# The first norm of a Swin block kernel placed in front of the preparation of all weights, with own buffers and a second queue for the loads

## The reference

```python
xl = roll(layernorm(x over channels) * n1w + n1b, (-3, -3))
xw = windows of 7 x 7 tokens                      # 16 * 64 windows of 49 tokens
q, k, v = xw @ qkv_w.T + qkv_b                    # 6 heads of 32
out = softmax(q k^T * 32**-0.5) v
out = out @ proj_w.T + proj_b                     # windows undone, rolled back
h = layernorm(out) * n2w + n2b
h = gelu(h @ fc1_w.T + fc1_b) @ fc2_w.T + fc2_b   # hidden size 768
return h + x
```

## Time and profile before

| | |
|---|---|
| median of 3 runs | 3201.64 us |
| the profiled execution | 3201.47 us |
| its span, first to last instruction | 3199.7 us |
| mean granted TensorE clock, of full speed | 0.998 |
| busy: PE, ACT, DVE, POOL | 98%, 93%, 78%, 32% |
| chain of work that ended last | PE 97%, DVE 1%, SP's queue 1%, ACT 1% |
| bytes moved by DMA | 129.30 MB, mean 40 GB/s |

### The profile page before, as it was taken

How to read it: one execution, slowest core, us unless ns; L and a number is a source line. 1 busy time by engine, 2 the same in 40 slices (tenths; PEclk the granted TensorE clock), 3 DMA queues, 4 the chain that set the end, 5 groups by cost and what they waited for, 6 DMA issues and landing times.

```text
span 3199.7 us, 76844 instructions
## 1 busy us (share of the span) xinstructions
PE 3133.7 (98%) x28076; PEld 3046.4 (95%) x28076; DVE 2501.2 (78%) x7214; ACT 2978.5 (93%) x5498; POOL 1019.0 (32%) x1288
## 2 busy tenths in 40 slices
PE   3999999999999999999999999999999999999998
PEld 3899999999999999999999999999999999999998
DVE  4787788788778878877887887787788788778876
ACT  1899999999999999999999999999999999999997
POOL 0233333333333333333333333333333333323332
PEclk9999999999999999999999999999999999999999
DMA  2112112111211211121121121112111111211211
GB/s 63 21 40 46 38 39 43 42 38 40 46 37 39 43 42 38 41 45 37 39 44 41 39 43 42 38 40 46 38 39 43 42 38 40 46 37 39 43 33 28
DMA packets 458709, 129.30 MB, mean 40 GB/s; under 512 B 392803, under 2 KB 458084, under 8 KB 458340
## 3 DMA queue, kind: packets, MB, share of 16 engines
q1 hardware_dynamic: 458340, 124.39, 18.4%
HBM read 47.20 MB, written 38.54 MB: 27 GB/s over the span
## 4 chain that ended last, share of the span: by engine, by line
PE 97%; DVE 1%; SPq 1%; ACT 1%; DMA 0%; issue 0%; POOL 0%; POOLq 0%; DVEq 0%; ACTq 0%
PE psum L547 8%; PE psum L304 7%; PE psum L306 6%; PE psum L305 6%; PE psum L307 6%; PE psum L308 6%; PE psum L526 6%; PE psum L517 4%; PE psum L506 4%; PE psum L507 4%; PE psum L508 4%; PE psum L518 4%; PE psum L480 4%; PE psum L532 4%; PE psum L314 3%; PE psum L318 3%
## 5 line engine op out<-in xcount | busy, mean ns | idle before, releaser
L1056 POOL TENSOR_TENSOR ve<-mv,eps 98x4 f32<-98x4 f32 x256 | 133.4, 521 | 1854.2 <-DVE mv L863 1854.2
L868 DVE TENSOR_SCALAR xn<-psum,mv,rs 98x192 f32<-98x192 f32 x1024 | 460.6, 471 | 38.3 <-POOL rs L1058 34.1
L676 ACT ACTIVATE hh<-psum,b 128x392 fp32r<-128x392 f32 x768 | 452.7, 590 | 30.1 <-PE psum L518 6.3
L891 DVE TENSOR_TENSOR x_l<-psum,x_h 128x392 fp32r<-128x392 f32 x256 | 140.6, 549 | 391.6 <-ACT x_h L649 391.6
L679 ACT ACTIVATE hf<-psum,b 128x392 f32<-128x392 f32 x768 | 438.3, 589 | 3.1
L857 DVE BATCH_NORM_STATS2 st<-psum 98x6 f32<-98x192 f32 x1024 | 324.9, 348 | 104.3 <-PE psum L460 103.0
L1070 POOL TENSOR_TENSOR pr<-pr,rc 98x294 f32<-98x294 f32 x512 | 373.4, 738 | 52.5 <-DVE rc L933 52.5
L897 DVE TENSOR_TENSOR hl<-hf,hh 128x392 fp32r<-128x392 f32 x640 | 361.1, 564 | 8.1 <-ACT hf L679 8.1
L676 ACT ACT_TABLE_LOAD x253 | 324.6, 1283 | 4.5
L688 ACT ACT_TABLE_LOAD x252 | 323.3, 1283 | 4.5
L304 PE MATMUL psum<-x_h,w_mh 128*128 128x392 f32 x768 | 295.0, 384 | 1.7 <-ACT hf L679 1.2
(11 more groups left out here) (134 smaller groups left out, 10129.2 us busy)
## 6 DMA issues: line engine op xcount, KB each, us to landing
vbd<-vs SPq DMA_DIRECT2D x1024, 36.8 KB
xt<-in_x SPq DMA_DIRECT2D x112, 194.5 KB, 2.7
out<-xt SPq DMA_DIRECT2D x112, 194.5 KB, 2.0
xt<-in_x SPq DMA_DIRECT2D x112, 97.2 KB, 2.5
out<-xt SPq DMA_DIRECT2D x112, 97.2 KB, 2.2
xt<-in_x SPq DMA_DIRECT2D x112, 48.2 KB, 2.3
xt<-in_x SPq DMA_DIRECT2D x256, 0.8 KB, 2.0
xt<-in_x SPq DMA_DIRECT2D x128, 1.5 KB, 2.2
```

The lines of the kernel that those rows point to most:

```text
L676: nc.scalar.activation(hh[:, m % HB, :], bank("fc1", m)[:, 0:T], ACT.Gelu, bias=b1[:, m:m + 1]).then_inc(s_hh, 1)
L868: nc.vector.tensor_scalar(xn[ln][:, j // 2, j % 2 * C:j % 2 * C + C], ln_chunk(("ln1", "ln2")[ln], j), mv[ln][:, j, 0:1], rs[ln][:, j:j + ...
```

## The change

SP first loads x of unit 0 and the main rows of the qkv weights, then x of unit 1, the projection weights, the second norm's vectors, the remaining biases, and x of units 2 to 6. ACT issues 28 DMAs of its own at its start: the first norm's vectors, the other rows of the qkv weights, the qkv bias, and the two hidden layers' weights. Each weight has its own raw buffers, so `s_rawfree` goes. PE starts with `to_tokens` of unit 0. The qkv bias products stand behind the first `x1_channels`, and the waits for clears, for `wq` and for `bq`, `bk` behind them. The hidden bias products stand behind `x1_channels` of unit 1, in PSUM bank 1 (last used by tile 3 of qkv of unit 0), and PE waits behind them for `s_bias` 3. PE waits for all weights at the first `project`. On DVE the whole weight preparation (`weights`) stands behind the low part of `x1` of unit 0, and `b1` behind that of unit 1. ACT waits for clears and for `bq`, `bk` behind the high part of `x1` of unit 0. Four clears move from DVE to POOL.

Removed lines that only undo the passages described above are left out here, and so are the two helpers `norm_vector` (three DMAs for one norm vector) and `qkv_columns` (offsets of the six column groups).

```diff
@@ -50,7 +52,8 @@
 PA = 4 * W - SHIFT
 PB = T - SHIFT
-SMALL = 16 * (12 + 6 + 4 + MT)
+SMALL = 16 * 6
+REST = 16 * (6 + 4 + MT)
@@ -121,8 +124,10 @@
         pb_hi = sb("pb_hi", [1, CR + C], F32R)
         b1 = sb("b1", [128, MT])
         b2 = sb("b2", [128, 2])
-        raw_m = sb("raw_m", [128, NF])
-        raw_r = sb("raw_r", [128, NF])
+        raw_q = [sb(f"raw_q_{p}", [128, NQ]) for p in ("m", "r")]
+        raw_p = [sb(f"raw_p_{p}", [128, CR + C]) for p in ("m", "r")]
+        raw_1 = [sb(f"raw_1_{p}", [128, NF]) for p in ("m", "r")]
...
+        spare_0 = next(b for b in range(8) if b not in (BANK_OF["x1", 0], BANK_OF["x1", 1]))
+        x1_at = next(k for k, use in enumerate(BANK_USES) if use[:2] == ("x1", 1))
+        ran = [(name, i, bank, t - lag) for t in range(LAGS + 1)
+               for k, (name, i, bank, lag) in enumerate(BANK_USES) if t >= lag and (t - BANK_USES[x1_at][3], k) <= (1, x1_at)]
+        last_use = {bank: (k, name, i, v) for k, (name, i, bank, v) in enumerate(ran)}
+        spare_1 = min(range(8), key=lambda bank: last_use.get(bank, (-1,))[0])
+        before_hidden_bias = last_use[spare_1][1:] if spare_1 in last_use else (None, 0, 0)
@@ -348,38 +377,23 @@
                     sp.dma_start(of[b, 0:CM, px:px + n], xt[:, i, 0, at:at + n]).then_inc(s_st[i], 16)
                     sp.dma_start(of[b, CM:C, px:px + n], xt[0:CR, i, 1, at:at + n]).then_inc(s_st[i], 16)
+            load(0, 0)
+            for at, c0, m in qkv_columns():
+                sp.dma_start(raw_q[0][:, at:at + m], qkv_wt[0:CM, c0:c0 + m]).then_inc(s_raw[0], 16)
+            load(0, 1)
+            for d0, c0, m in ((0, CM, CR), (CR, 0, C)):
+                sp.dma_start(raw_p[0][:, d0:d0 + m], proj_wt[0:CM, c0:c0 + m]).then_inc(s_raw[1], 16)
                 for h in range(2):
+                    sp.dma_start(raw_p[1][h * CR:(h + 1) * CR, d0:d0 + m], proj_wt[CM:C, c0:c0 + m]).then_inc(s_raw[1], 16)
+            for vec, cols in ((n2w, 4), (n2b, 6)):
+                norm_vector(sp, vec, cols, s_rest)
             for m in range(MT):
+                sp.dma_start(b1[:, m:m + 1], fc1_b[m * 128:(m + 1) * 128].rearrange("(p a) -> p a", a=1)).then_inc(s_rest, 16)
+            sp.dma_start(pb[:, 0:CR], proj_b[CM:C].rearrange("(a c) -> a c", a=1)).then_inc(s_rest, 16)
+            sp.dma_start(pb[:, CR:CR + C], proj_b.rearrange("(a c) -> a c", a=1)).then_inc(s_rest, 16)
+            sp.dma_start(b2[:, 0:1], fc2_b[0:CM].rearrange("(p a) -> p a", a=1)).then_inc(s_rest, 16)
+            sp.dma_start(b2[0:CR, 1:2], fc2_b[CM:C].rearrange("(p a) -> p a", a=1)).then_inc(s_rest, 16)
...
-            for i in range(AHEAD):
+            for i in range(2, AHEAD):
@@ -434,20 +447,34 @@
                 for done, back, per, n in latest.values():
                     pe.wait_ge(done, nth(u + back, per, n))
+            def bias_products():
+                pe.wait_ge(s_small, SMALL)
+                pe.wait_ge(s_raw[0], 16 * 18)
+                for t, (c0, m) in enumerate(QKV_TILES):
+                    ps = psum[0:m, spare_0, t:t + 1]
+                    nc.tensor.matmul(ps, raw_q[0][:, c0:c0 + m], nwb[:, 2:3], start=True, stop=False)
+                    last = nc.tensor.matmul(ps, raw_q[1][0:CR, c0:c0 + m], nwb[0:CR, 3:4], start=False, stop=True)
+                last.then_inc(s_bias_mm, 1)
+                pe.wait_ge(s_zero, 1)
+                pe.wait_ge(s_zero_qk, 4)
+                pe.wait_ge(s_split, 1)
+                pe.wait_ge(s_bias, 2)
+            def hidden_bias_products():
+                name, i, v = before_hidden_bias
+                if name is not None:
+                    done, v, per, n = last_read(name, i, v)
+                    pe.wait_ge(done, nth(v, per, n))
+                pe.wait_ge(s_rest, REST)
+                pe.wait_ge(s_raw[2], 16 * 3)
+                for m in range(MT):
+                    ps = psum[:, spare_1, m:m + 1]
+                    nc.tensor.matmul(ps, raw_1[0][:, m * 128:(m + 1) * 128], nwb[:, 6:7], start=True, stop=False)
+                    last = nc.tensor.matmul(ps, raw_1[1][0:CR, m * 128:(m + 1) * 128], nwb[0:CR, 7:8], start=False, stop=True)
+                last.then_inc(s_bias_mm, 1)
+                pe.wait_ge(s_bias, 3)
@@ -460,6 +487,9 @@
                 nc.tensor.transpose(bank("ln1", c)[0:TP, CM:2 * CM], xt[:, k, 1, TP * c:TP * c + TP], ident[:, :]).then_inc(s_pe["ln1"], 1)
             def project(u, j):
+                if u == 0 and j == 0:
+                    pe.wait_ge(s_split, 4)
                 if j % 2 == 0:
                     claim(u, [("ln2", j // 2)], (s_lo["o"], 2, 1))
                 ps = ln_chunk("ln2", j)
@@ -482,6 +512,10 @@
             def x1_channels(u, g):
                 to_channels("x1", u, g, in_row)
+                if g == 1 and u == 0:
+                    bias_products()
+                if g == 1 and u == 1:
+                    hidden_bias_products()
@@ -642,8 +676,18 @@
         @block.scalar
         def _(act):
-            act.wait_ge(s_zero, 1)
-            act.wait_ge(s_bias, 3)
+            norm_vector(act, n1w, 0, s_small)
+            norm_vector(act, n1b, 2, s_small)
+            for at, c0, m in qkv_columns():
+                for h in range(2):
+                    act.dma_start(raw_q[1][h * CR:(h + 1) * CR, at:at + m], qkv_wt[CM:C, c0:c0 + m]).then_inc(s_raw[0], 16)
+            for at, c0, m in qkv_columns():
+                t, r = next((k, at - a) for k, (a, n) in enumerate(QKV_TILES) if a <= at < a + n)
+                act.dma_start(bq[r:r + m, t:t + 1], qkv_b[c0:c0 + m].rearrange("(p a) -> p a", a=1)).then_inc(s_bq, 16)
+            act.dma_start(raw_1[0][:, :], fc1_wt[0:CM, :]).then_inc(s_raw[2], 16)
+            for h in range(2):
+                act.dma_start(raw_1[1][h * CR:(h + 1) * CR, :], fc1_wt[CM:C, :]).then_inc(s_raw[2], 16)
+            act.dma_start(raw_2[:, :, :], fc2_wt.rearrange("(m p) n -> p m n", p=128)).then_inc(s_raw[3], 16)
             def copy(dst, src, done):
                 nc.scalar.activation(dst, src, ACT.Copy).then_inc(done, 1)
@@ -666,8 +710,15 @@
                     biased(HI_LO[name][dst][0:m], src, bq[0:m, g:g + 1], s_hi[name])
                 else:
                     copy(HI_LO[name][dst][0:m], src, s_hi[name])
+                if name == "x1" and g == 1 and u == 0:
+                    act.wait_ge(s_zero, 1)
+                    act.wait_ge(s_zero_qk, 4)
+                    act.wait_ge(s_bias, 2)
             def gelu_hi(u, m):
+                if u == 0 and m == 0:
+                    act.wait_ge(s_bias, 3)
                 if m >= HB:
                     act.wait_ge(s_pe["fc2"], nth(u, MT, m - HB))
@@ -796,28 +847,19 @@
             for t in (wp[3],):
                 nc.vector.memset(t[:].bitcast(F32), 0.0)
-            for t in (qm, km, qr, kr, vbd, pr, pt, mv[0], mv[1], half_k):
+            for t in (vbd, pr, pt, mv[0], mv[1], half_k):
                 nc.vector.memset(t[:], 0.0)
             nc.vector.memset(o_b[CR:128, :].bitcast(F32), 1.0).then_inc(s_zero, 1)
+            def split(n, w, raw, cols, nw, scaled):
+                sm_, sr_ = raw
                 dve.wait_ge(s_raw[n], 16 * (18, 6, 3)[n])
                 if nw is not None:
                     if n:
                         dve.wait_ge(s_split, n)
+                    nc.vector.tensor_scalar(scl_m[:, 0:cols], sm_[:, 0:cols], nwb[:, nw:nw + 1], None, ALU.mult).then_inc(s_scaled, 1)
+                    nc.vector.tensor_scalar(scl_r[:, 0:cols], sr_[:, 0:cols], nwb[:, nw + 1:nw + 2], None, ALU.mult).then_inc(s_scaled, 1)
                     scaled += 2
                     dve.wait_ge(s_scaled, scaled)
                     sm_, sr_ = scl_m, scl_r
...
+                return scaled
+            def weights():
+                dve.wait_ge(s_small, SMALL)
+                dve.wait_ge(s_zero, 1)
+                for h in range(4):
+                    nc.vector.memset(half_k[DH * h:DH * h + DH, h % 2:h % 2 + 1], 1.0)
+                scaled = split(0, wq, raw_q, NQ, 0, 0)
+                dve.wait_ge(s_bq, 16 * 6)
+                dve.wait_ge(s_bias_mm, 1)
+                for t, (c0, m) in enumerate(QKV_TILES):
+                    last = nc.vector.tensor_tensor(bq[0:m, t:t + 1], bq[0:m, t:t + 1], psum[0:m, spare_0, t:t + 1], ALU.add)
+                last.then_inc(s_bias, 1)
+                dve.wait_ge(s_bias, 1)
+                nc.vector.tensor_scalar(bk[:, :], half_k[:, :], bq[:, 3:4], None, ALU.mult).then_inc(s_bias, 1)
+                dve.wait_ge(s_rest, REST)
+                nc.vector.tensor_copy(pb_hi[:, :], pb[:, :]).then_inc(s_scaled, 1)
+                scaled += 1
+                dve.wait_ge(s_scaled, scaled)
+                nc.vector.tensor_copy(wp[3][64:65, :], pb_hi[:, :].bitcast(F32))
+                nc.vector.tensor_tensor(wp[3][96:97, :], pb[:, :], pb_hi[:, :].bitcast(F32), ALU.subtract)
+                scaled = split(1, wp, raw_p, CR + C, None, scaled)
```

(50 more changed lines are left out.)

25 lines of the change are left out of this document (removed).

## The result

The changed kernel takes 3173.39 us (median of 4 runs, 3172.68 to 3175.39), the kernel before in the same comparison 3202.27 us: a ratio of 0.9913, 95% interval 0.9901 to 0.9926, or 28.9 us less. The forecast was 3172, 29.1 us less. The interval reaches from 24 to 32 us, so the agreement to 0.2 us says no more than that the forecast lies well inside it. The profiled execution has a span of 3170.9 us against 3199.7 before, so the traces differ by the same amount as the runs.

The account below looks back on a forecast made before the run. PE, busy throughout 120 to 3150 us, was taken to bound the kernel, so gains at the start count one for one: 34.5 - 4.9 - 0.5 = 29.1 us off 3201.47, forecast 3172, range 3167 to 3184.

Parts of the forecast that it names:

- Step 1: x and its norm at the start: x lands near 6 us; clears and this chain cost nothing.
- Step 2: ACT's queue at the start: its issues take 16.2 us, so ACT is free at 16.9.
- Step 3: First qkv product on PE: begins at 24.2 us in place of 61.61, 37.4 us ahead.
- Step 4: Rest of the weights on DVE: small loads landed at 24.8, unit 1 statistics about 34.1; 34.5 of 37.4 us left.
- Step 5: Hidden bias products before qkv of unit 1: 4.9 us at the low clock, plus 0.5 for the stage before.
- Step 6: SP's loop: eight issues after x loads land at 49.3 us, weighted sum needs them at 52.7 or later; costs nothing.
- The queues slow each other: Rival, SP and ACT issuing together: each issue takes up to twice as long, 3189 us; chance 15%.
- The doubling: Each issue taking twice as long while both queues run, if the descriptor generator serves one queue at a time; 3189 us.
- Late landings: Rival, loads at the start: a small load lands after 4.5 us instead of 2.0, giving 3175 us; chance 6%.
- The clock was up: Rival, PE's clock stays high at the start: hidden bias products cost only 1.7 us, giving 3169; chance 12%.
- PE's pace in the middle: Rival, PE's long stretch: moved SBUF tiles slow PE's stream by more than 1%; at 2%, 3233 us; chance 3%.

Follow-up runs that it names:

- e8: e7 with SP's block moves of unit 0's values issued behind the loads of x of unit 3, ahead of units 4 to 6; 3159.87 us.
- e6: The changed kernel with ten of ACT's 28 issues (qkv bias, hidden layers' weights) behind ACT's high part of x1 of unit 0; 3172.24 us.
- e5: The changed kernel with the two hidden layers' weights prepared later on DVE, in two of its idle stretches; 3168.86 us.
- e9: The changed kernel with only SP's block moves of unit 0's values put ahead of the loads of x of units 4 to 6; 3171.48 us.
- e7: The changed kernel with e5 and e6 joined, projection's bias row and weights loaded before x of unit 1, bias products halved behind units 1 and 2; 3170.17 us.
- e4: The changed kernel with the twelve hidden bias products moved into PE's idle stretch between the halves of to_tokens of unit 1; 3169.26 us.

## Why the prediction was right

*What bounds the kernel.* Right. PE is busy all through the middle, and in every run the lead at the start came out at the end. The first qkv product of unit 2, before and after:

```profile
98.06 0.45 PE L304 MATMUL psum<-x_h,wq_mh 128*128 128x392 f32 x1 [2.56 <-DVE x_r L891]
```

```profile
68.92 0.69 PE L311 MATMUL psum<-x_h,wq_mh 128*128 128x392 f32 x1 [2.55 <-DVE x_r L944]
```

There the changed kernel is 29.1 us ahead and e8 43.1 (54.94), with spans 28.8 and 43.1 us shorter; in the other runs lead and span agree within 1.3 us. The spans are of single executions on several chips: for e8 the medians, taken on one chip, show 40.2.

*Step 1.* Right: first transpose at 6.22, channels at 13.15, and neither the clears nor this chain was waited for.

*Step 2.* Right in kind, 1.0 us short: ACT is free at 17.93, not 16.9. The term at fault is the twelve 64-row issues, 7.75 for 6.8. The one-queue run has them at 7.62 on a lone queue, so hardly any of this is the queues slowing each other: I took the pace from a row of two such issues between others.

*Step 3.* Right: 7.5 us from ACT's table load to the first qkv product, 7.3 in the sum; 25.44 for 24.2, nearly all by step 2's miss.

*Step 4.* Right, 1.2 us short. DVE went on behind the small loads at 25.99, not 24.8: SP's issues ended at 23.93, not 23.2, and from the start of the last one (23.46) it was 2.5 us, not 2.0. The statistics came at 35.29 for 34.1, and of the lead 33.4 was left for 34.5. All of that is step 4's own: DVE was done with the qkv weights at 25.18, so step 2's miss lay inside its wait. e6 shows that this and not ACT was the path; e5, that taking the work out of DVE's way frees 3 us.

*Step 5.* The cost was mis-sized and the level wrong. From the statistics to qkv of unit 1 the lead fell by 3.8 us (33.4 to 29.5), not 5.4. The low clock came earlier than I had put it, right behind PE's stop, and slowed the stage (1.2 us where I had 0.5: the channels end at 44.6, where the lead is 32.1), and it was over when the products began: twelve in 4.0 us (44.60 to 48.56), a pass pair at 0.31 and only the last near the low pace, not 6.24 at 0.52. So the products cost 2.6 us (3.96 + 0.25 of waiting - 1.61) where I had 4.9, the stage 0.7 more than I had. Together that is 1.6 us too much cost, and it hid the 1.2 us missing in step 4. That the total came out so close is partly luck: the path was the one foreseen, but the clock level was wrong and two sizes erred in opposite directions.

*Step 6.* Right for the changed kernel, as e9 shows, though not by the reckoning given. The eight moves began at 41.75 and their issues ended at 48.96 (7.21 us, not 6.3). And I had looked only at the weighted sum, which came at 58.10; DVE's copy of unit 1's values, at 54.71, needs the moves too and comes first. It is the wait that e7 ran into.

*The rivals.* The queues slow each other a little: SP's first twelve issues took 7.47 us beside ACT's and 6.51 without (starts 8.20 and 7.24), its forty 23.2 against 21.7, ACT's 28 took 17.2 against 16.9. That is 1.5 us and no doubling, so the two queues did not take turns for whole issues. The Trainium skill, Perfetto Trace Analysis, section "DMA Instruction — HWDGE (DVE, Sync)", says that the descriptor generator is locked for one issue and shared between sequencers. The doubling that I had drawn from it did not come; whether a lock held for a small part of each issue made the 1.5 us, no run here shows. The other rule, the Trainium skill's DMA: Bandwidth & Descriptors, section "Issuing engines are not separate DMA queues", agrees in what a second queue saves and differs in the size: issue time was worth 15.0 us here. Late landings came at 0.5 us, not 2.5. The clock was up for the products (granted 0.93), but not ahead of them (0.50). PE's pace in the middle did not drop: 27067 recorded matmuls in the 3000 us, 27016 before.

## What to carry to other kernels

In a kernel whose long middle is bound by one engine, count the issues on each queue and the instructions of each engine up to that engine's first work: each microsecond on the path there is worth one, and here an order that puts the needed work first gained 10.5 us, as much as own buffers (9.5) or a second queue (8.9). Follow the path past the first product: a piece of preparation moved behind it can stand in the way of the next unit, and then bringing the first product forward gains nothing (e6). After each gain, cost the covered queues anew, with every instruction that waits for them and not only the one you have in mind; what had some 4 us to spare was the next wait (e7).

## What was not expected of the hardware

The clock fell behind a stretch in which PE hardly idled: in e4 PE worked from 25.44 to 36.0 with a single gap of 0.24 us, some 3.7 us of it on the hidden bias products (busy for all of 32 to 36), and the granted clock of the next stretch was 0.58. In e5 it fell in the middle of the same products, in the changed kernel at the last of them. No run separates these products from the other work around them, so the cause stays open.

Where the clock falls differs between kernels in which PE does the same there. e9 differs from the changed kernel in SP's queue alone, had the same stop of PE (3.96 for 3.39), and qkv of unit 1 started at 46.98 in place of 48.81: its first transposes behind the stop ran at the high level (0.42 for a pair that took 0.66), no wait was gone, and the medians are alike. Some 2 us of a start are of that kind.

ACT issues DMAs while its own ACTIVATE runs (timeline of e7):

```profile
13.19 0.33 ACTq L691 DMA_DIRECT2D bq<-in_qkv_b  x1
13.25 0.50 ACT L698 ACTIVATE x_h<-psum 128x392 fp32r<-128x392 f32 x1
13.56 0.48 ACTq L691 DMA_DIRECT2D bq<-in_qkv_b  x1
```

Here issues placed behind an eviction in the program began beside it.
